# Sparsemax candidates taken one row earlier, and layer 0's softmax denominators summed in four column bands

## The reference, cut to what matters

```python
# layer 0: 16 heads of 64, per head
k = apply_rope(k, cos, sin)
attn = softmax(clip(q @ k.T * 64**-0.5, -11, 11))     # 512 x 1024
out = attn @ v
# layer 1: 16 heads of 16, per head
scores = q @ k.T * 16**-0.5                           # 512 x 1024
attn = clip(scores - tau(scores), 0)   # sparsemax: tau makes each row sum to 1
out = attn @ v
```

## Time and profile before

| | us |
|---|---|
| median of 3 runs (range) | 3668.53 (3667.57 to 3669.78) |
| profiled execution | 3675.92 |
| its span | 3674.1 |
| PE busy | 2806.2 (76%) |
| DVE busy | 2203.0 (60%) |
| ACT busy | 1432.8 (39%) |

### The profile page before, as it was taken

The page is one execution under the profiler, slowest core; times in us unless marked ns, Lnnn a source line. Parts: engine busy times, 40 slices in busy tenths (PEclk is TensorE's granted clock), DMA queues, the critical chain, the costliest instruction groups (busy, mean ns, idle before and its releaser), DMA issues. The chain is left out here.

```text
span 3674.1 us, 39781 instructions
## 1 busy us (share of the span) xinstructions
PE 2806.2 (76%) x12862; PEld 1807.2 (49%) x12862; DVE 2203.0 (60%) x4947; ACT 1432.8 (39%) x2218; POOL 326.4 (9%) x145
## 2 busy tenths in 40 slices
PE   2999998345566666666999967787787697799588
PEld 2444444232233333336888854554543576454377
DVE  4666674766777677624555444556564555676377
ACT  1444442213777777732222212212143232166221
POOL 0000000001000000001112101011110111200021
PEclk7999999676777777777999988998888798799699
DMA  1000000024011110001011010000241110632010
GB/s 55 13 13 13 13 9 13 23 72 139 1 24 24 24 29 24 1 8 69 34 51 51 26 37 12 1 0 0 73 104 25 44 40 14 188 70 53 19 48 29
DMA packets 49516, 136.62 MB, mean 37 GB/s; under 512 B 8664, under 2 KB 20960, under 8 KB 44768
## 3 DMA queue, kind: packets, MB, share of 16 engines
q1 hardware_dynamic: 49376, 135.01, 12.4%
HBM read 106.28 MB, written 28.31 MB: 37 GB/s over the span
## 5 line engine op out<-in xcount | busy, mean ns | idle before, releaser
L1679 PE MATMUL ps<-m1e_x_part_s,m1e_up_part_s 128*128 128x512 f32 x1296 | 298.0, 391 | 22.0 <-POOL m1e_up_part_s L1775 15.9
L1449 ACT ACTIVATE l1a_over_s<-l1a_sc_s,l1a_minus_step_s 128x1024 bf16<-128x1024 f32 x256 | 290.0, 1138 | 3.0 <-DVE l1a_minus_step_s L1323 1.7
L1679 PEld LDWEIGHTS ps<-m1e_x_part_s,m1e_up_part_s 128*128 128x128 f32 x1296 | 243.8, 189 | 74.1 <-issue 23.7
L1263 DVE MAX8 l1a_cand_s<-ps 128x8 f32<-128x128 f32 x1024 | 213.3, 284 | 72.0 <-PE ps L1158 68.8
L1191 PE MATMUL ps<-l1a_probs_s,l1h_v_s 128*32 128x256 f32 x1024 | 126.4, 583 | 157.9 <-ACT l1a_probs_s L1457 156.3
L1722 ACT ACTIVATE m1e_act_out_s<-ps 128x512 f32<-128x512 f32 x108 | 64.7, 599 | 346.8 <-PE ps L1679 346.8
L1435 ACT ACTIVATE l1a_sc_s<-ps,l1a_minus_tau_s 128x1024 f32<-128x1024 f32 x128 | 142.0, 1112 | 142.2 <-DVE l1a_minus_tau_s L1292 53.4
L976 DVE TENSOR_REDUCE l3a_shift_s<-ps 128x1 f32<-128x1024 f32 x128 | 150.4, 1220 | 51.9 <-PE ps L893 51.9
L538 DVE TENSOR_SCALAR l0a_probs_s<-l0a_probs_s 128x1024 f32<-128x1024 f32 x128 | 88.5, 691 | 150.5 <-ACT l0a_probs_s L605 150.0
L1158 PE MATMUL ps<-l1h_ka_s,l1h_qa_s 128*128 128x512 f32 x256 | 132.8, 564 | 55.4 <-DVE l1a_cand_s L1263 45.2
L605 ACT ACTIVATE l0a_probs_s<-ps 128x1024 f32<-128x1024 f32 x128 | 131.0, 1024 | 104.6 <-PE ps L455 103.4
(11 more groups left out here) (530 smaller groups left out, 5837.7 us busy)
## 6 DMA issues: line engine op xcount, KB each, us to landing
m1ew_up_s<-m_up SPq DMA_DIRECT2D x9, 1536.0 KB, 6.2
l1h_ka_s<-l_k_parts SPq DMA_DIRECT2D x16, 512.0 KB, 7.9
l3h_ka_s<-l_k_parts SPq DMA_DIRECT2D x16, 512.0 KB, 8.2
m1ew_down_s<-m_down SPq DMA_DIRECT2D x9, 768.0 KB, 4.1
l0a_w_s<-l_w SPq DMA_DIRECT2D x16, 384.0 KB, 2.9
m3ew_up_s<-m_up SPq DMA_DIRECT2D x6, 768.0 KB, 4.2
l1h_qa_s<-l_q_parts SPq DMA_DIRECT2D x16, 256.0 KB, 6.0
l_v_groups<-l1p_v_all_s SPq DMA_DIRECT2D x4, 1024.0 KB, 9.7
```

The costliest lines, as they stand in the source:

```text
L1263: ins = nc.vector.max(cand[:, r, 8 * (c + j * 4):8 * (c + j * 4) + 8], ps[:, A0 + f % 2, c * P:(c + 1) * P])
L1449: nc.scalar.activation(over[:, done % 2, :], sc[:, r, :], ACT.Relu, bias=minus_step[:, r:r + 1], accum_out=total[:, i, r:r + 1]).then_inc( ...
L1679: ins = nc.tensor.matmul(ps[:, 2 * (u % 2) + way, :], up_parts[a][:, k, way, c, :], x_parts[b][:, k, half * BANK:(half + 1) * BANK], start ...
```

## The change

Layer 0: `probs` has eight slots. The matmuls with ones are done at odd t only, for two steps at once: four matmuls of 32 columns each, one for each of (t - 1, head 0), (t - 1, head 1), (t, head 0), (t, head 1), into four bands of 32 partitions of bank 7. Once a group, PE multiplies ACT's copy of that bank with a new constant 128 x 128 matrix `pair_sum`, which adds the bands of one head and spreads the sum over its 64 rows, again into bank 7 (`denominators`, after t = 2 of the next group); ACT copies the result to `spread_den` (`copy_denominators`, after the exponential of t = 2), from which `finish` takes the reciprocal.

Layer 1: `sc` holds ten rows instead of eight, used in rotation, so ACT's first sums wait for `settled` before their third row instead of before their first. Row 0's scores and candidates of unit u + 2 are moved to PE's t = 3 of iteration u and into DVE's `settle(u)`, between the step and the wait for the turned worst error; those of all other rows keep their places' order, one row later. `probabilities` has three buffers instead of four.

```diff
@@ constants
+            pool.memset(pair_sum[:, :], 0.0).then_inc(filled, 1)
+            both = pair_sum[:, :].rearrange("p (h c) -> p h c", h=2)
+            for part in range(2):
+                pool.wait_ge(made, 4 + part)
+                pool.affine_select(out=both, in_=both, compare_op=ALU.not_equal, fill=1.0, base=-64 * part,
+                                   pattern=[[-32, 2], [0, 64]], channel_multiplier=1).then_inc(made, 1)
@@ rope_attention
-    SLOTS = 4
+    SLOTS = 8
@@ PE, value_product
-                    pe.wait_ge(den_copied, n + 1)
+                if t == 1:
+                    pe.wait_ge(den_copied, 2 * n + 1)
...
-                for h in range(2):
-                    ins = nc.tensor.matmul(ps[64 * h:64 * h + 64, 7, :], ones[:, 0:64],
-                                           probs[:, t % SLOTS, h * NQ:(h + 1) * NQ], start=(t == 0), stop=(t == NC_ - 1))
-                ins.then_inc(pv_done, 1)
+                if t % 2 == 1:
+                    for i in range(4):
+                        ins = nc.tensor.matmul(ps[32 * i:32 * i + 32, 7, :], ones[:, 0:32],
+                                               probs[:, (t - 1 + i // 2) % SLOTS, i % 2 * NQ:(i % 2 + 1) * NQ],
+                                               start=(t == 1), stop=(t == NC_ - 1))
+                    ins.then_inc(pv_done, 2)
+            def denominators(n):
+                pe.wait_ge(den_copied, 2 * n + 2)
+                nc.tensor.matmul(ps[:, 7, :], pair_sum[:, :], den[:, :], start=True, stop=True).then_inc(den_made, 1)
@@ PE, step
+                    if last is not None and t == 2:
+                        denominators(n - 1)
@@ DVE, finish
-                nc.vector.reciprocal(rden[:, :], den[:, :]).then_inc(rden_ready, 1)
+                nc.vector.reciprocal(rden[:, :], spread_den[:, :]).then_inc(rden_ready, 1)
@@ ACT
+            def copy_denominators(n):
+                act.wait_ge(den_made, n + 1)
+                act.wait_ge(rden_ready, n)
+                nc.scalar.activation(spread_den[:, :], ps[:, 7, :], ACT.Copy).then_inc(den_copied, 1)
...
+                    if t == 2 and last is not None:
+                        copy_denominators(n - 1)
@@ sparse_attention
+    KEPT = ROWS + 2
+    def kept(u, r):
+        return (ROWS * u + r) % KEPT
-        sc = s.sb("sc", [P, ROWS, nk])
+        sc = s.sb("sc", [P, KEPT, nk])
-        probs = s.sb("probs", [P, 4, 2 * NQ])
+        probs = s.sb("probs", [P, 3, 2 * NQ])
@@ PE
+            first_row(1, 0)
-                        first_row(u + 1, r - 2)
+                        first_row(u + 1, r - 1)
-                    if u + 1 < UNITS and t < 4:
-                        first_row(u + 1, 4 + t)
+                    if u + 1 < UNITS and t < 3:
+                        first_row(u + 1, 5 + t)
...
+                    if u + 2 < UNITS and t == 3:
+                        first_row(u + 2, 0)
@@ DVE, settle
+                if u + 2 < UNITS:
+                    candidates(u + 2, 0)
                 dve.wait_ge(worst_turned, u + 1)
@@ ACT, first_sums
-                if u > 0:
-                    act.wait_ge(settled, u)
                 for r in range(ROWS):
+                    if u > 0 and r == KEPT - ROWS:
+                        act.wait_ge(settled, u)
@@ ACT, probabilities
-                if NC_ * u + t >= 4:
-                    act.wait_ge(pv_done, NC_ * u + t - 3)
+                if NC_ * u + t >= 3:
+                    act.wait_ge(pv_done, NC_ * u + t - 2)
```

More of the change, by code:

```diff
@@ L94, in link, with constants @@
         self.wait()
-def constants(nc, ident, ones, slot_pick, spread):
+def constants(nc, ident, ones, slot_pick, spread, pair_sum):
     with Stage(nc, "const") as s:
@@ L338, in _, with rope_attention @@
             dve.wait_ge(added, TQ)
-def rope_attention(nc, name, ps, ones, q_t, ctx_t, w_dram, cos_dram, sin_dram, o_all):
+def rope_attention(nc, name, ps, ones, pair_sum, q_t, ctx_t, w_dram, cos_dram, sin_dram, o_all):
     DH = 64
@@ L369, in rope_attention @@
         o_raw, rden = s.sb("o_raw", [P, NQ]), s.sb("rden", [P, NQ])
-        den = s.sb("den", [P, NQ])
+        den, spread_den = s.sb("den", [P, NQ]), s.sb("spread_den", [P, NQ])
         tables, negated = s.sem("tables"), s.sem("negated")
@@ L385, in rope_attention @@
         pv_done = s.sem("pv_done")
-        o_copied, den_copied = s.sem("o_copied"), s.sem("den_copied")
+        o_copied, den_copied, den_made = s.sem("o_copied"), s.sem("den_copied"), s.sem("den_made")
         rden_ready, o_done = s.sem("rden_ready"), s.sem("o_done")
@@ L494, in step @@
                     value_product(n, p, NC_ - 1)
+                    denominators(n)
             over_groups(pe, first, step)
@@ L636, in step @@
                     copy_output(n)
+                    copy_denominators(n)
             over_groups(act, first, step)
@@ L1348, in settle @@
                         for r in range(ROWS):
-                            more.link(nc.vector.tensor_scalar(over[:, 2, :], sc[:, r, :], step[:, r:r + 1], 0.0,
+                            more.link(nc.vector.tensor_scalar(over[:, 2, :], sc[:, kept(u, r), :], step[:, r:r + 1], 0.0,
                                                               ALU.is_gt, ALU.add, accum_out=count[:, r:r + 1]))
-                            more.link(nc.vector.scalar_tensor_tensor(over[:, 2, :], sc[:, r, :], step[:, r:r + 1],
+                            more.link(nc.vector.scalar_tensor_tensor(over[:, 2, :], sc[:, kept(u, r), :], step[:, r:r + 1],
                                                                      zero[:, :].to_broadcast([P, nk]), ALU.subtract, ALU.max,
@@ L1401, in _ @@
             first_threshold(0)
+            candidates(1, 0)
             for u in range(UNITS):
@@ L1405, in _ @@
                 if u + 1 < UNITS:
-                    for r in range(ROWS // 2):
+                    for r in range(1, 5):
                         candidates(u + 1, r)
@@ L1409, in _ @@
                 if u + 1 < UNITS:
-                    for r in range(ROWS // 2, ROWS):
+                    for r in range(5, ROWS):
                         candidates(u + 1, r)
@@ L1448, in sums @@
                         act.wait_ge(summed, done - 1)
-                    nc.scalar.activation(over[:, done % 2, :], sc[:, r, :], ACT.Relu, bias=minus_step[:, r:r + 1],
+                    nc.scalar.activation(over[:, done % 2, :], sc[:, kept(u, r), :], ACT.Relu, bias=minus_step[:, r:r + 1],
                                          accum_out=total[:, i, r:r + 1]).then_inc(summed, 1)
@@ L2467, in build @@
         slot_pick, spread = sb("slot_pick", [P, 60]), sb("spread", [P, 6, P], F32R)
+        pair_sum = sb("pair_sum", [P, P])
         x = sb("x_rows", [P, TQ, D])
@@ L2472, in by_feature @@
             return A[name + "_f"]
-        constants(nc, ident, ones, slot_pick, spread)
+        constants(nc, ident, ones, slot_pick, spread, pair_sum)
         load_x(nc, A["x"], x)
@@ L2508, in build @@
                 o_all = sb("l0_o_all", [P, 8, NT], stack=l0)
-                rope_attention(nc, "l0a", ps, ones, q_t, c_t, A["l0_w"], A["l0_cos"], A["l0_sin"], o_all)
+                rope_attention(nc, "l0a", ps, ones, pair_sum, q_t, c_t, A["l0_w"], A["l0_cos"], A["l0_sin"], o_all)
                 project_out(nc, "l0o", ps, o_all, 8, A["l0_wo"], A["L0_xattn_bo"], x)
```

14 lines of the change are left out of this document (7 added, 7 removed).

## The result

| us | before | after |
|---|---|---|
| median of the runs | 3668.05 (3663.14 to 3669.78, 4 runs) | 3608.74 (3607.32 to 3613.51, 4 runs) |
| profiled execution: own time, span | 3675.9, 3674.1 | 3607.32, 3605.3 |
| mean granted clock of TensorE | 0.854 | 0.867 |

The ratio is 0.9843 with an interval of 0.9826 to 0.9860: 59.3 us less where 39.8 were forecast.

The account below looks back on a forecast made before the run. PE bounds layer 0's attention; layer 1 is a loop of waits with no engine full. Layer 0 -29.0, layer 1 -11.6 and constants +0.8 sum to -39.8 us: 3668.5 to 3628.7 us, likeliest range 3614 to 3639, wider 3612 to 3648.

Parts of the forecast that it names:

- Layer 0: Layer 0's attention, bound by PE: fewer ones matmuls, less width changes, added product and end, -29.0 us in all.
- the 0.15 that I took: Layer 0, PE's change from 64 to 32 columns: 0.15 us each, 64 times, 9.6 us lost.
- 0.86 in the sum: Layer 0, each second ones pair left out frees a bare PE turn of 0.86 us, 55.0 us in all.
- The added product: Layer 0, PE's multiplication by pair_sum once a group: 0.86 us each, 13.8 us lost over 16.
- R4: Rival, layer 0: the four 32-column bands do not run together; 13.5 us slower, 3682 us; chance 3%.
- R3: Rival, layer 0: ACT's second copy is late and PE's value product waits; 16 us, 3645 us; chance 12%.
- where I had counted 1.7: Layer 0's last group: two pairs left out only make PE wait for DVE's clip; 1.7 us not gained.
- Constants: Before the first load: one more fill and two selections on 128 x 128, +0.8 us (0.6 to 1.2).
- This 0.91 us is all that goes: Layer 1, only PE's wait for ACT before row 2 vanishes: 15 units x 0.91 = 13.7 us won.
- R1: Rival, layer 1: ACT's whole wait for the shift comes back; 43.5 us instead of 13.7, 3599 us; chance 8%.
- the moved row: Layer 1, eight MAX8 fit DVE's wait for the turned error: 0.7 us lost in 13 units, 1.4 in unit 0.
- R2: Rival, layer 1: moved candidates delay the settling by 1.68 us a unit; 23.5 instead of 2.1, 3650 us; chance 9%.

Follow-up runs that it names:

- e9: The kernel after, unchanged, measured again on one chip with three variants: 3610.30 us, ratio 0.9830 to before.
- e5: The kernel before, with eight unread matmuls on PE ahead of its wait for the shift, all waits kept: 3651.03 us, ratio 0.9936.
- e11: The kernel after, with eight unread matmuls on PE ahead of its wait for the shift: 3604.55 us, ratio 0.9815 to before.
- e3: The kernel before, with layer 1's ten-row sc and three buffers of probabilities, candidates unmoved: 3639.25 us, ratio 0.9919.
- e6: The kernel after, with PE's third row held back until DVE has written the shift's second part: 3634.78 us, ratio 0.9896.
- e4: The kernel before, with row 0's candidates moved and three buffers of probabilities, sc still eight rows: 3671.06 us, ratio 1.0007.
- e10: The kernel after, with all candidate rows where they were in the kernel before: 3610.16 us, ratio 0.9834 to before.
- e7: The kernel after, with nine rows of sc in place of ten: 3616.43 us, ratio 0.9844.

## Why the prediction was right or wrong

**Layer 0, right in its terms, with one small wait missing.** -27.3 against -29.0 (-28.7 in e9). In a step with a group of four, value pair and group take 1.01 + 1.00 = 2.01 us from start to start, where value pair and ones pair took 0.91 + 0.95 = 1.86: the change from 64 to 32 columns costs 0.15, the 0.15 that I took. The Trainium skill (TensorEngine Tiling (Array Packing), Key Properties) has it that a change of tiling mode drains the engine; this trace agrees for 64 to 32 columns in so far as the change costs time, 0.15 us. In a step whose pair is left out the value pair takes 1.01 us alone, 0.85 less than the 1.86, against 0.86 in the sum. The added product takes 349.74 - 349.17 = 0.57 us, and the score matmul behind it 350.37 - 349.74 = 0.63 where it takes 0.34 otherwise: 0.86, as taken. R4 falls with the same rows: the bands run together. R3 falls with the waits: ACT waits about 1 us for the product, 16.8 us in 16 times, and none of PE's own waits between 90 and 590 us is for ACT's second copy. At the end the second copy puts DVE 586.20 - (583.70 + 0.59) = 1.9 us behind ACT's first, 1.8 were taken.

1.7 us are missing, and two executions of one kernel differ by up to 1.4. But a regular part of it shows in the groups: from one copy to `o_raw` to the next a group takes 31.21 us (33.05 before), 1.84 less, where my terms give 4 x 0.86 - 4 x 0.15 - 0.86 = 1.98. The step with the value projection (L446) ahead of the scores takes 0.13 us longer than before in most groups, and PE waits 0.3 us behind it, 13 times, where the kernel before has that wait once; in the two groups in which that step is as short as before a group takes 31.05. I had no term for this wait, and what it waits for stays open. DVE had the room that I said: PE itself waits for DVE's clip once, 1.3 us, in the last group, where I had counted 1.7.

**Constants.** +1.0 against +0.8, within the 0.6 to 1.2 given.

**Layer 1, the step that failed** is "This 0.91 us is all that goes: row 0 is then long read", with "15 units x 0.91 = 13.7 us won". The wait did go, in every unit. But I took the rows behind it as they were, and their durations stood at 1.2 GHz: 1.22 us for two matmuls in the earlier trace rows. With the gap gone PE stays at 2.4 GHz in ten of 15 units, the rows are then paced by DVE's candidates (waits of 0.29 ahead of L1188) and no longer by PE, and the first sums end 2.6 us earlier behind the shift, of which 0.91 is the gap.

The term that failed is thus the price of the clock, which I put at nothing. e5 and e11 take the two apart, since both have the clock at 1.00 in 14 of 15 units: a unit takes 44.4 us in the kernel before, 42.8 with the clock raised and the gap kept (e5), 41.8 with the gap gone as well (e11). The clock is worth 1.6 us a unit and the gap 1.0, so the 0.91 was sized about right. Over the stage that is 24.4 us of clock (e5) and 13.2 more for the gap (752.3 - 739.1 in e11), against my 13.7 for the gap alone. The kept rows by themselves measure 33.5 us in e3, less than the sum of the two, with 1.00 in eight of 15 units. With that in place of 13.7 my sum would be 39.8 + 33.5 - 13.7 = 59.6 us, where the medians give 59.3; that it comes so close is luck, since the stage is known to some 4 us only.

The clue stood in the rows I quoted, and I wrote it down as a reason for R1: "shorter PE gaps might bring the full clock earlier". I had given that thought no price of its own. R1 itself fell. It gives 41.8 us for a unit and the trace has 41.86, but not by its mechanism: ACT's third row waits 1.11 us for PE's rows, and e6, in which ACT has its two rows of lead, loses most of the gain (24 to 28 of 31 to 35 us). The number agreed by chance, and units by themselves would have confirmed the wrong rival.

The page TensorE: Matmul & The Clock Gate of the Trainium skill (A second HAM failure mode: psum-queue depth-cycling) describes the like for another kernel: PE idles briefly but often between groups of matmuls, and its clock goes up and down between two levels. The traces here agree: 0.50 or 0.51 in every unit of the kernel before, and both levels from unit to unit in the kernel after and in e6.

**Layer 1, the moved row.** Right: cost near nothing, hidden by DVE's wait. DVE reads the worst error as soon as the last MAX8 is done, at 1192.60, with no wait; PE had turned it at 1192.03 + 0.28 = 1192.31, and before the reading followed 0.1 us behind that, so 0.2 us of this unit are lost by it. R2 would need the whole 1.68. e4 with +2.5 us in the median, an interval of -0.03% to +0.17%, and e10 say the same. But it wins nothing either.

**The range.** It held rivals by waits, and no case in which PE's rows run at the other level. From the earlier trace rows such a case has its price: these rows of the first 6.5 us behind the shift at 1.00 in place of 0.50.

## What to carry to other kernels

Read the granted clock of the stretch in which the critical loop stands before pricing a wait on PE: here the gap itself cost about 1 us a unit and the low clock of the rows behind it another 1.6. Where a loop's paced matmuls run at 1.2 GHz behind short idles of PE, try to close one of them, or put matmuls that nobody reads into the wait (into partitions of a PSUM bank that nobody uses). Then look at the rows behind them in every unit: 14 fillers that left 4.26 us of a hole open gave nothing, 24 with eight more gave 15.4 us, and even those left five of 15 units with rows at 1.2 GHz. And when an edit's unit time matches a rival, look at which engine waits before believing it.

## What the runs showed of the hardware

- TensorE's mean granted clock in the 6.5 us behind the shift, over the first 15 units: 0.50 or 0.51 in all where PE had idled 1.9 to 2.6 us and idled 0.91 us more a little later (before); 0.50 to 0.56 in eight, 0.69 to 0.74 in six and 1.00 in one where the second idle was 0.68 us (e6); 1.00 in ten or six, by execution, where there was no second idle (after, e9); 1.00 in 14 where unread matmuls filled most of the first idle, with a second idle of 1.0 us (e5) or without (e11).
- In the kernel before the fall stands ahead of the second idle, within 0.3 us of the shift. The lower level then lasts some 7 us; with a fall at the same place and no second idle some 3.5 us (e9, e7).
- Two score matmuls of 512 elements each took 1.22 us together at the lower level and 0.70 us at the higher.
- Unread matmuls beside a waiting PE cost the loop nothing in e5: sixteen records take 1.94 us, end before the shift comes, and delay nothing behind them.
- Four matmuls of 32 columns with 512 elements each take one turn together, 1.00 us; a step with them behind a pair of 64 columns is 0.15 us longer than a step with a second pair of 64.
